# Cross attention and a mixture of experts on one core: score work of the second group moved into the first step, and operand forms changed

## The chip, the cores and the metric

The kernel runs on one core of one Trainium2 chip. The metric is the device time of one execution in microseconds (us), lower is better. The kernel before took 248.23 us (median of three runs, 245.85 to 248.69). Engines are named as in the profile: PE (TensorE), DVE (VectorE), ACT (ScalarE), POOL (GpSimd) and SP (SyncE, which here only issues DMAs).

## The reference, cut to what matters

```python
# x, ctx: (16, 128, 128) = batch, sequence, features
x = x + xattn(layernorm(x), ctx, ctx, Wq, bq, Wk, bk, Wv, bv, Wo, bo)
x = x + ffn(layernorm(x), Wr, Wg, Wu, Wd, Sg, Su, Sd)

def xattn(q, k, v, ...):                     # 16 heads of 8 features
    scores = einsum('bhid,bhjd->bhij', Q, K) / sqrt(8) + alibi_bias(128)
    return einsum('bhij,bhjd->bhid', softmax(scores), V) @ Wo.T + bo

def ffn(x, ...):                             # 16 experts of 64, top 2, and a shared one of 128
    probs = softmax(x @ Wr); top_p, top_i = top_k(probs, 2)
    routed = sum over e of (silu(x @ Wg[e]) * (x @ Wu[e])) @ Wd[e] * c[e]
    return routed + (silu(x @ Sg) * (x @ Su)) @ Sd
```

## The kernel before

The batch of 16 sequences is cut into eight groups of two (NG = 8, NB = 2 sequences b of 128 rows, T = 256). Each engine has its own program, written out by hand, and semaphores join them. Work is pipelined over groups: a step handles up to four of them at once, `step(f, a, p, q, abuf)`: the experts of group f, the attention of group a = f+1, the q/k/v products of p = f+2 and the first layer norm of q = f+3. The first step is `step(None, 0, 1, 2, 0)`, attention of group 0 with no expert work beside it; then `run_steps` issues `step(0, 1, 2, 3, 1)`, four steps in a hardware loop, two more, and a tail for group 7. Within a step the order on each engine is the order of the code. Nothing on an engine overtakes an instruction that waits.

Attention of a group and sequence b runs as: `scores(a, b, g)` on PE, four heads at a time (g = 0..3) into the two PSUM banks `ps_s`; `row_max` on DVE for each (L881), so that PE can't be more than two ahead; `max_high` (L887) and `max_low` (L891) split the 16 maxima into two float16 parts, `nsplit`; `shift_T` on PE transposes them, `shift_copy` on ACT copies them and `shift_rows` sends them by DMA as two extra rows of the stacked queries (`s_nm`); only then `scores_T` on PE forms the transposed and shifted scores, ACT takes exponentials (L668), `weigh_values` and `values_T` form the weighted values, `row_sums` and `normalise` divide, `attention_T` and `project_out` project, and `residual1` adds the residual (L914). Then `norm2_stats`, `norm2_mean` on DVE, the power -1/2 on POOL (L1179, L1183) and `norm2` on DVE (L933, `x2n`) give the input of the experts. Sequence 0's `norm2` is the step's last but three DVE call; sequence 1's comes at the start of the next step, and `expert_in_T` on PE waits for it.

The expert part: `up(f, c)` on PE for nine chunks c in high and low float32r parts of the weights (`wg_hi`, `wg_lo` and so on), tanh on ACT, `gate` and `hidden` on DVE, multiplication by the routing weights on POOL (`weigh_experts`, L1211: `hid` times `crep`, both in SBUF, 128x512), `down` on PE. `weigh_experts(f, 0)` stands on POOL between the two `inverse_deviation2` calls. The routing weights go to DRAM (`weights_out`, a DMA from ACT's queue, L676) and come back spread over the partitions (`spread_weights`, SP). The low parts of the weights are formed once, in the first step (`weights_low`, L1002 to L1004, DVE). `keep_clock` issues PE transposes whose results are unused.

Which operands lie where matters below: `x_all`, `x1_all`, `mv2`, `rstd2`, `nmax`, `nsplit`, `zero`, `hid`, `crep`, `xb` and the weights are in SBUF; what begins with `ps_` is in PSUM.

## Time and profile before

| | before |
|---|---|
| median of three runs | 248.23 us (245.85 to 248.69) |
| the profiled execution, own time | 247.91 us |
| its span | 246.1 us |
| PE busy / DVE / ACT / POOL | 222.8 / 181.0 / 111.2 / 65.9 us |
| granted PE clock, mean | 0.986 of full |

The span is what the trace covers; 1.8 us of the execution's time lie around it. Times in the rows count from the span's start. A row of the timeline gives start, duration, engine, line, operation, output and inputs, and in brackets how long the engine was idle before it and what ended the wait. The first step is about 16.6 to 37.9 us, the second 37.9 to 62.3, and each step after that takes 26.5 us or a little more.

### The profile page before, as it was taken

The page shows a single profiled execution, that of the slowest core. Times are in us where ns is not written, and L with a number is a line of the kernel's source. Part 1 is how long each engine was busy: PE and PEld are TensorE (multiplying, and loading weights), DVE is VectorE, ACT ScalarE, POOL GpSimd, SP SyncE. Part 2 cuts the span into 40 slices and gives each one's busy share as a digit, 9 for nine tenths or more (in the row PEclk, how much of TensorE's full clock was granted, in tenths as well). Part 3 has the DMA queues.
Part 4 walks back from the last instruction along what each step waited for, and adds up shares of the span by engine and source line. Part 5 has one row for each costly group of instructions (what it writes and reads, how often), then busy time and mean ns, then how long its engine had stood idle before and what let it go on. Part 6 is the DMA issues. An engine that isn't in the chain of part 4 may idle for free.

```text
span 246.1 us, 6073 instructions
## 1 busy us (share of the span) xinstructions
PE 222.8 (91%) x1979; PEld 180.0 (73%) x1979; DVE 181.0 (74%) x644; ACT 111.2 (45%) x260; POOL 65.9 (27%) x119
## 2 busy tenths in 40 slices
PE   2886978899899998999899989999999889989995
PEld 2773556668698777877787869877887669768985
DVE  4699348965997589847996589658983899356882
ACT  8574445365325632464336432563256323752320
POOL 3500014010741047013811074105700380017000
PEclk9998699999999999999999999999999999999999
DMA  5651792425024510624051602460164300260000
GB/s 153 187 99 62 151 289 79 112 45 160 1 72 75 147 52 23 122 79 119 0 127 23 186 0 76 68 175 17 32 113 106 93 0 4 51 149 0 3 21 21
DMA packets 13078, 20.23 MB, mean 82 GB/s; under 512 B 2800, under 2 KB 9440, under 8 KB 12544
## 3 DMA queue, kind: packets, MB, share of 16 engines
q1 hardware_dynamic: 11856, 18.52, 31.1%
q10 hardware_dynamic: 1200, 1.43, 2.0%
q8 instruction: 12, 0.20, 0.3%
q14 instruction: 10, 0.08, 0.1%
HBM read 16.03 MB, written 3.78 MB: 81 GB/s over the span
## 4 chain that ended last, share of the span: by engine, by line
PE 44%; issue 30%; POOL 11%; DVE 8%; DMA 4%; ACT 1%; POOLq 0%; DVEq 0%; SPq 0%; ACTq 0%
PE ps_m L504 8%; PE ps_up L478 7%; POOL hid L1211 6%; PE ps_pv L413 4%; DVE nmax L881 4%; PE ps_st L384 4%; PE ps_st L394 4%; PE ps_up L483 3%; PE ps_pv L420 2%; POOL rstd L1183 2%; DMA stacks_sb<-qk_dram 2%; PE ps_up L292 2%; PE ps_st L446 1%; DMA ident<-in_c_ident 1%; DVE tg L987 1%
## 5 line engine op out<-in xcount | busy, mean ns | idle before, releaser
L987 DVE SCALAR_TENSOR_TENSOR tg<-th,ps_up 128x256 f32<-128x256 f32 x72 | 29.8, 414 | 29.3 <-ACT th L713 29.3
L668 ACT ACTIVATE probs<-ps_st 128x512 f32<-128x512 f32 x64 | 38.1, 598 | 25.1 <-PE ps_st L394 20.3
L713 ACT ACTIVATE th<-ps_up 128x256 f32<-128x256 f32 x72 | 27.6, 384 | 42.1 <-PE ps_up L483 42.0
L504 PE MATMUL ps_m<-wd_sb,hid 128*128 128x128 f32 x288 | 44.1, 280 | 0.6 <-DVE x_all L914 0.6
L881 DVE TENSOR_REDUCE nmax<-ps_s 128x4 f32<-128x512 f32 x64 | 42.6, 680 | 0.5 <-issue 0.4
L504 PEld LDWEIGHTS ps_m<-wd_sb,hid 128*128 128x128 f32 x288 | 37.6, 191 | 1.4 <-DVE x_all L914 1.0
L1211 POOL TENSOR_TENSOR hid<-hid,crep 128x512 f32<-128x512 f32 x28 | 35.1, 1274 | 3.8 <-DVE x2n L933 3.8
L993 DVE TENSOR_TENSOR hid<-tg,ps_up 128x256 f32<-128x256 f32 x72 | 29.8, 413 | 1.0
L478 PE MATMUL ps_up<-x_hi,wg_hi 128*128 128x256 f32 x72 | 26.6, 369 | 2.6 <-DVE hid L993 2.5
L351 PE MATMUL ps_s<-stacks_sb 96*128 96x128 f16 x256 | 23.8, 220 | 3.0 <-DVE nmax L881 2.5
L1179 POOL TENSOR_TENSOR ve<-mv,eps_sb 128x1 f32<-128x1 f32 x16 | 3.1, 192 | 84.7 <-DVE mv L926 84.7
L394 PE MATMUL ps_st<-stacks_sb 98*128 98x128 f16 x256 | 25.6, 225 | 0.0
L394 PEld LDWEIGHTS ps_st<-stacks_sb 98*128 98x128 f16 x256 | 19.1, 100 | 7.2 <-issue 0.9
L351 PEld LDWEIGHTS ps_s<-stacks_sb 96*128 96x128 f16 x256 | 16.5, 97 | 9.3 <-DVE nmax L881 6.5
L1171 POOL TENSOR_TENSOR ve<-mv,eps_sb 128x2 f32<-128x2 f32 x8 | 1.6, 195 | 70.7 <-DVE mv L840 70.7
L483 PE MATMUL ps_up<-x_lo,wg_hi 128*128 128x256 f32 x72 | 20.1, 279 | 0.0
L478 PE MATMUL ps_up<-x_hi,wg_lo 128*128 128x256 f32 x72 | 20.1, 279 | 0.0
L478 PE MATMUL ps_up<-x_hi,wu_hi 128*128 128x256 f32 x72 | 20.1, 279 | 0.0
L478 PE MATMUL ps_up<-x_hi,wu_lo 128*128 128x256 f32 x72 | 20.1, 279 | 0.0
L483 PE MATMUL ps_up<-x_lo,wu_hi 128*128 128x256 f32 x72 | 20.0, 278 | 0.0
L413 PE MATMUL ps_pv<-probs,v_aug 128*32 128x384 f32 (+1 forms) x256 | 17.1, 385 | 0.5 <-ACT probs L668 0.5
L478 PEld LDWEIGHTS ps_up<-x_hi,wg_hi 128*128 128x128 f32 x72 | 13.6, 190 | 4.8 <-DVE hid L993 2.4
(133 smaller groups left out, 442.3 us busy)
## 6 DMA issues: line engine op xcount, KB each, us to landing
crep<-cw_dram SPq DMA_DIRECT2D x28, 256.0 KB, 4.4
stacks_sb<-qk_dram SPq DMA_DIRECT2D x32, 128.0 KB, 3.7
qk_dram<-qk_parts SPq DMA_DIRECT2D x16, 128.0 KB, 1.8
out_y<-x_all SPq DMA_DIRECT2D x8, 128.0 KB, 4.0
wg_sb<-in_wgT ACTq DMA_DIRECT2D x1, 576.0 KB, 3.4
wu_sb<-in_wuT ACTq DMA_DIRECT2D x1, 576.0 KB, 3.4
wd_sb<-in_wd SPq DMA_DIRECT2D x1, 576.0 KB, 3.9
x_all<-in_x SPq DMA_DIRECT2D x2, 256.0 KB, 4.2
```

The source lines that it names most:

```text
L351: last = mm(bank[:, o:o + P], qs[buf][0:ZROWS, h, b * P:(b + 1) * P], ks[buf][0:ZROWS, h, b * P:(b + 1) * P], start=(g > 0), stop=True, sk ...
L394: last = mm(bank[:, o:o + P], ks[buf][:, h, b * P:(b + 1) * P], qs[buf][:, h, b * P:(b + 1) * P], start=first, stop=True, skip_group_check ...
L413: last = mm(ps_pv[32 * c:32 * c + 32, r * 3 * P:(r * 3 + n) * P], v_aug[:, b, r, c, :], probs[:, b, h * P:(h + n) * P], start=True, stop=T ...
L478: mm(ps_up[c % 2][:, k, :], w[:, c, :], x2_hi[:], start=(k == 0 and n == 0), stop=False, skip_group_check=True)
L483: last = mm(ps_up[c % 2][:, k, :], hi[:, c, :], x2_lo[:], start=False, stop=True, skip_group_check=True)
L504: last = mm(ps_dn[:, b * P:(b + 1) * P], hid[:, buf, c, b * P:(b + 1) * P], wd_sb[:, c, :], start=(c == 0 and b == 0), stop=(c == SHARED), ...
L668: fn(probs[:, b, g * HG * P:(g + 1) * HG * P], ps_st[g % 2][:], ACT.Exp).then_inc(exp_sb, 1)
L713: fn(th[:, c % 2, :], ps_up[c % 2][:, 0, :], ACT.Tanh, scale=0.5).then_inc(tanh_sb, 1)
L881: v.tensor_reduce(nmax[:, b, HG * g:HG * g + HG], ps_s[g % 2][:].rearrange("p (h j) -> p h j", h=HG), AX_X, ALU.max, negate=True).then_inc ...
L987: v.scalar_tensor_tensor(out=tg[:, c % 2, :], in0=th[:, c % 2, :], scalar=1.0, in1=ps_up[c % 2][:, 0, :], op0=ALU.add, op1=ALU.mult).then_ ...
L993: v.tensor_tensor(hid[:, buf, c, :], tg[:, c % 2, :], ps_up[c % 2][:, 1, :], ALU.mult).then_inc(hid_sb, 1)
L1211: g.tensor_tensor(h2, h2, c2, ALU.mult).then_inc(hc_sb, 1)
```

## The change

1. The first step (`first`) now also issues the score products of group 1 for (b, g) = (0,0) to (1,1) and the row maxima for (0,0) to (1,0), and group 1's first transposed maxima. The second step (`second`) issues what is left of them, so that group 1's scores no longer stand in front of and between the expert products of group 0. The order of the rest in the two steps changes with it. Group 1's value product goes to another PSUM bank (`ps_v1`, in `ps_up[0]`). More `keep_clock` transposes stand in the first step (1, 2, 2, 2, 3, 3 and 8 where before there were 6).
2. `weights_low` moves from DVE to POOL.
3. Both norms (`norm1`, `norm2`) become `scalar_tensor_tensor` with the reciprocal deviation as a second tensor (broadcast from one column) in place of `tensor_scalar` with two per-partition scalars; `max_high` becomes a `tensor_tensor` addition of a broadcast zero in place of a casting copy.
4. The DMA of the routing weights to DRAM is issued by SP in `spread_weights`, not by ACT.

From the third step on the order on PE and DVE is the same as before; only the forms of 3 and the issuer of 4 differ.

```diff
@@ run_steps
-            step(0, 1, 2, 3, 1)
+            second(0, 1, 2, 3, 1)
@@ SP
             def spread_weights(f):
+                sp.wait_ge(cwT_sb, f + 1)
+                sp.dma_start(cw_dram[f], cwT[:]).then_inc(s_cwd, 16)
                 sp.wait_ge(s_cwd, 16 * f + 16)
@@ ACT
-            def weights_out(f):
-                act.wait_ge(cwT_sb, f + 1)
-                act.dma_start(cw_dram[f], cwT[:]).then_inc(s_cwd, 16)
@@ PE
+            def first():
...
+                shift_T(0, 0)
+                scores(0, 1, 1, 0)
+                keep_clock(3)
+                project_v(1)
+                scores(0, 1, 2, 0)
+                keep_clock(3)
+                scores(0, 1, 3, 0)
+                keep_clock(8)
+                scores_T(0, 0, 0, 0)
+                shift_T(0, 1)
...
+                weigh_values(0, 0)
+                scores(1, 0, 0, 1)
+                scores_T(0, 1, 2, 0)
+                values_T(0, 0)
+                scores(1, 0, 1, 1)
+                scores_T(0, 1, 3, 0)
+                scores(1, 0, 2, 1)
+                attention_T(0, 0, None)
+                weigh_values(0, 1)
+                project_out(0, 0)
+                scores(1, 0, 3, 1)
+                values_T(0, 1)
+                scores(1, 1, 0, 1)
+                attention_T(0, 1, None)
+                scores(1, 1, 1, 1)
+                project_x(2)
+                project_out(0, 1)
+                shift_T(1, 0)
+
+            def second(f, a, p, q, abuf):
+                project_q(p)
+                project_k(p)
+                scores(a, 1, 2, abuf)
+                expert_in_T(f)
+                scores(a, 1, 3, abuf)
+                up(f, 0)
+                router(f)
+                up(f, 1)
+                shift_T(a, 1)
+                up(f, 2)
+                scores_T(a, 0, 0, abuf, f=f)
+                up(f, 3)
+                scores_T(a, 0, 1, abuf, p=p)
+                second_half(f, a, p, q, abuf)
@@ DVE
-                    last = v.tensor_scalar(xn[:, b, :], x_all[:, p * NB + b, :], mv1[:, b, 0:1], rstd1[:, b:b + 1],
-                                           ALU.subtract, ALU.mult)
+                    last = v.scalar_tensor_tensor(out=xn[:, b, :], in0=x_all[:, p * NB + b, :], scalar=mv1[:, b, 0:1],
+                                                  in1=rstd1[:, b:b + 1].to_broadcast([P, P]), op0=ALU.subtract, op1=ALU.mult)
...
-                v.tensor_copy(nsplit[:, b, 0, :], nmax[:, b, :]).then_inc(nh_sb, 1)
+                v.tensor_tensor(nsplit[:, b, 0, :], nmax[:, b, :], zero[:].to_broadcast([P, H]), ALU.add).then_inc(nh_sb, 1)
...
-                v.tensor_scalar(x2n[:, b, :], x1_all[:, a * NB + b, :], mv2[:, b, 0:1], rstd2[:, b:b + 1],
-                                ALU.subtract, ALU.mult).then_inc(x2n_sb, 1)
+                v.scalar_tensor_tensor(out=x2n[:, b, :], in0=x1_all[:, a * NB + b, :], scalar=mv2[:, b, 0:1],
+                                       in1=rstd2[:, b:b + 1].to_broadcast([P, P]), op0=ALU.subtract,
+                                       op1=ALU.mult).then_inc(x2n_sb, 1)
@@ POOL, called in the first step between copy_ctx(1) and inverse_deviation1(2)
+            def weights_low():
+                pool.wait_ge(act_setup, 4)
+                g.tensor_tensor(wg_lo[:], wg_sb[:], wg_hi[:].bitcast(F32), ALU.subtract).then_inc(lo_sb, 1)
+                g.tensor_tensor(wr_lo[:], wr_sb[:], wr_hi[:].bitcast(F32), ALU.subtract).then_inc(lo_sb, 1)
+                pool.wait_ge(act_setup, 5)
+                g.tensor_tensor(wu_lo[:], wu_sb[:], wu_hi[:].bitcast(F32), ALU.subtract).then_inc(lo_sb, 1)
```

Two places of the order, as the programs have it (operation, output and inputs by name, elements of the output; a row may stand for several alike). DVE in the first step, from group 0's first row maxima to the first reciprocal of row sums, before:

```order
L881 TENSOR_REDUCE nmax<-ps_s 128x4 x4
L887 CAST nsplit<-nmax 128x16
L891 TENSOR_TENSOR nsplit<-nmax,nsplit 128x16
L862 SCALAR_TENSOR_TENSOR qk_parts<-ps_st,bqk_sb,qk_parts 128x256 x2
L1002 TENSOR_TENSOR wg_lo<-wg_sb,wg_hi 128x1152
L1003 TENSOR_TENSOR wu_lo<-wu_sb,wu_hi 128x1152
L1004 TENSOR_TENSOR wr_lo<-wr_sb,wr_hi 128x16
L896 RECIPROCAL rden<-ps_pv 128x16
```

(these begin with sequence 1's maxima), and after the change, from the end of sequence 0's maxima on:

```order
L966 TENSOR_TENSOR nsplit<-nmax,zero 128x16
L970 TENSOR_TENSOR nsplit<-nmax,nsplit 128x16
L941 SCALAR_TENSOR_TENSOR qk_parts<-ps_st,bqk_sb,qk_parts 128x256 x2
L960 TENSOR_REDUCE nmax<-ps_s 128x4 x4
L966 TENSOR_TENSOR nsplit<-nmax,zero 128x16
L970 TENSOR_TENSOR nsplit<-nmax,nsplit 128x16
L960 TENSOR_REDUCE nmax<-ps_s 128x4
L975 RECIPROCAL rden<-ps_pv 128x16
```

The low parts of group 1's keys and queries (`qk_parts`) moved ahead of sequence 1's four row maxima, the three weight subtractions left the engine, and a row maximum of group 1 stands ahead of the reciprocal. POOL in the first step, after the change:

```order
L1315 COPY ctx_g<-ctx_all 128x256
L1319 TENSOR_TENSOR wg_lo<-wg_sb,wg_hi 128x1152
L1320 TENSOR_TENSOR wr_lo<-wr_sb,wr_hi 128x16
L1322 TENSOR_TENSOR wu_lo<-wu_sb,wu_hi 128x1152
L1282 TENSOR_TENSOR ve<-mv,eps_sb 128x2
```

Before, the deviation of group 2 (`ve`) followed the copy directly.

## Rows read from the trace of the kernel before

**Rows 1.** The page's busy times: us, share of the span, instructions

```profile
PE 222.8 (91%) x1979; PEld 180.0 (73%) x1979; DVE 181.0 (74%) x644; ACT 111.2 (45%) x260; POOL 65.9 (27%) x119
```

**Rows 2.** Busy time by stretch: PE, PEld, DVE, ACT, POOL; then clock, DMA share, GB/s

```profile
16.60:23.60 7.00, 4.58 (x41) 2.93 (x41) 6.75 (x15) 4.18 (x5) 0.00 (x0) 0.90 0.27 88
23.60:37.90 14.30, 12.61 (x103) 8.30 (x103) 6.58 (x28) 6.53 (x13) 1.70 (x4) 0.81 0.81 215
37.90:62.30 24.40, 22.16 (x203) 16.68 (x202) 18.69 (x77) 13.01 (x31) 4.09 (x11) 1.00 0.36 85
88.80:115.30 26.50, 25.50 (x237) 20.90 (x237) 20.95 (x79) 11.85 (x30) 8.62 (x15) 1.00 0.34 80
```

**Rows 3.** Timeline, all engines, the seam between two steps of the loop

```profile
88.55 1.26 POOL L1211 TENSOR_TENSOR hid<-hid,crep 128x512 f32<-128x512 f32 x1
88.62 1.27 DVE L933 TENSOR_SCALAR x2n<-x_all,mv,rstd 128x128 f32 x1 [0.20 <-POOL rstd L1183]
88.65 0.49 PE L433 MATMUL ps_m<-wT,attnT 128*128 128x128 f32 x2
...
89.82 0.28 DVE L914 TENSOR_TENSOR x_all<-ps_m,xb 128x128 f32 x1
...
91.32 0.40 PE L351 MATMUL ps_s<-stacks_sb 96*128 96x128 f16 x4 [0.15 <-DVE nmax L881]
...
93.36 0.39 PE L478 MATMUL ps_up<-x_hi,wg_hi 128*128 128x256 f32 x1 [0.38 <-DVE hid L993]
```

**Rows 4.** Timeline, POOL and DVE, a few us later in the same step

```profile
92.08 3.75 POOL L1211 TENSOR_TENSOR hid<-hid,crep 128x512 f32<-128x512 f32 x3 [0.54 <-DVE x2n L933]
94.86 0.99 DVE L887 CAST nsplit<-nmax 128x16 f16<-128x16 f32 x1
95.79 0.46 POOL L1193 TENSOR_TENSOR xb<-x_all,bo_rep 128x128 f32<-128x128 f32 x1
96.11 0.17 DVE L891 TENSOR_TENSOR nsplit<-nmax,nsplit 128x16 f16<-128x16 f32 x1
```

**Rows 5.** One line's instructions: shortest, median, longest in ns, first and last start

```profile
L933 DVE TENSOR_SCALAR x2n<-x_all,mv,rstd x16: 335/406/1287, 37.9 to 224.0; 128x128 f32<-128x128 f32 x8, 128x128 f32 x8
L887 DVE CAST nsplit<-nmax x16: 174/174/1002, 20.0 to 206.9; 128x16 f16<-128x16 f32 x16
L891 DVE TENSOR_TENSOR nsplit<-nmax,nsplit x16: 167/174/175, 20.2 to 207.1; 128x16 f16<-128x16 f32 x16
```

**Rows 6.** Timeline of the first step and the start of the second

```profile
22.29 1.16 ACT L717 ACTIVATE wu_hi<-wu_sb 128x1152 fp32r<-128x1152 f32 x1 [1.35 <-issue]
22.93 0.17 DVE L887 CAST nsplit<-nmax 128x16 f16<-128x16 f32 x1
23.23 0.87 DVE L862 SCALAR_TENSOR_TENSOR qk_parts<-ps_st,bqk_sb,qk_parts 128x256 f16<-128x256 f32 x2
...
24.02 1.35 DVE L1002 TENSOR_TENSOR wg_lo<-wg_sb,wg_hi 128x1152 fp32r<-128x1152 f32 x1
...
29.02 0.39 PE L384 MATMUL ps_st<-slope_hi,dist 128*128 128x512 f16 x1
...
32.26 0.26 DVE L896 RECIPROCAL rden<-ps_pv 128x16 f32<-128x16 f32 x1 [5.55 <-PE ps_pv L420]
...
39.98 0.47 DVE L933 TENSOR_SCALAR x2n<-x_all,mv,rstd 128x128 f32<-128x128 f32 x1 [0.37 <-POOL rstd L1183]
40.37 0.68 DVE L881 TENSOR_REDUCE nmax<-ps_s 128x4 f32<-128x512 f32 x1
```

**Rows 7.** Timeline of the second step: a shift DMA and the routing DMA

```profile
49.85 0.62 ACTq L672 DMA_DIRECT2D stacks_sb<-nmT  x1
...
50.04 0.36 PE L478 MATMUL ps_up<-x_hi,wg_hi 128*128 128x256 f32 x1
...
52.31 0.36 ACTq L676 DMA_DIRECT2D cw_dram<-cwT  x1
...
52.85 0.38 PE L384 MATMUL ps_st<-slope_hi,dist 128*128 128x512 f16 x1 [0.23 <-DMA stacks_sb<-nmT]
```

More of the change, by code:

```diff
@@ L588, in _ @@
             keep_clock(36)
-            step(None, 0, 1, 2, 0)
-            run_steps(pe, step)
+            first()
+            run_steps(pe, step, second)
             f, last = NG - 1, (NG - 1) % 2
@@ new lines, in first @@
+            def first():
+                qk_high(1)
+                shift_copy(0, 0)
+                shift_rows(0, 0, 0)
+                up_weights_high()
+                shift_copy(0, 1)
+                shift_rows(0, 1, 0)
+                for b in range(NB):
+                    for g in range(NHG):
+                        exponential(0, b, g)
+                        if (b, g) == (1, 1): values_copy(0, 0)
+                attention_copy(0, 0)
+                values_copy(0, 1)
+                attention_copy(0, 1)
+                x_T(2)
+                shift_copy(1, 0)
+                shift_rows(1, 0, 1)
@@ new lines, in second @@
+            def second(f, a, p, q, abuf):
+                qk_high(p)
+                x2_high(f)
+                tanh(f, 0)
+                act.wait_ge(s_wd, 16)
+                fn(wd_sb[:], wd_sb[:], ACT.Copy, scale=0.5).then_inc(wd_half, 1)
+                tanh(f, 1)
+                shift_copy(a, 1)
+                shift_rows(a, 1, abuf)
+                router_exp(f)
+                tanh(f, 2)
+                exponential(a, 0, 0)
+                tanh(f, 3)
+                second_half(f, a, q)
@@ L795, in _ @@
             fill(ks[1][ZROWS:AROWS], ones16)
-            step(None, 0, 1, 2, 0)
-            run_steps(act, step)
+            first()
+            run_steps(act, step, second)
             f = NG - 1
@@ new lines, in first @@
+            def first():
+                for g in range(NHG):
+                    row_max(0, 0, g)
+                max_high(0, 0)
+                max_low(0, 0)
+                qk_low(1, 1)
+                qk_low(1, 0)
+                for g in range(NHG):
+                    row_max(0, 1, g)
+                max_high(0, 1)
+                max_low(0, 1)
+                row_max(1, 0, 0)
+                row_sums(0, 0)
+                normalise(0, 0)
+                row_max(1, 0, 1)
+                norm1_stats(2)
+                norm1_mean(2)
+                row_max(1, 0, 2)
+                residual1(0, 0)
+                row_max(1, 0, 3)
+                norm2_stats(0, 0)
+                max_high(1, 0)
+                norm2_mean(0, 0)
+                max_low(1, 0)
+                row_sums(0, 1)
+                normalise(0, 1)
+                row_max(1, 1, 0)
+                norm1(2)
+                norm2(0, 0)
+                residual1(0, 1)
+                norm2_stats(0, 1)
+                norm2_mean(0, 1)
+                values(1)
@@ new lines, in second @@
+            def second(f, a, p, q, abuf):
+                row_max(a, 1, 1)
+                norm2(f, 1)
+                row_max(a, 1, 2)
+                x2_low(f)
+                row_max(a, 1, 3)
+                max_high(a, 1)
+                max_low(a, 1)
+                router_max(f)
+                gate(f, 0)
+                router_shift(f)
+                hidden(f, 0, 1 - abuf)
+                qk_low(p, 1)
+                qk_low(p, 0)
+                gate(f, 1)
+                hidden(f, 1, 1 - abuf)
+                route(f, 0)
+                route(f, 1)
+                gate(f, 2)
+                route(f, 2)
+                hidden(f, 2, 1 - abuf)
+                second_half(f, a, p, q, abuf)
@@ new lines, in step @@
+            def step(f, a, p, q, abuf):
+                row_max(a, 0, 0)
+                norm2(f, 1)
+                row_max(a, 0, 1)
+                gate(f - 1, 8)
+                hidden(f - 1, 8, abuf)
+                x2_low(f)
+                row_max(a, 0, 2)
+                row_max(a, 0, 3)
+                max_high(a, 0)
+                gate(f, 0)
+                max_low(a, 0)
+                hidden(f, 0, 1 - abuf)
+                if p is not None: qk_low(p, 1)
+                row_max(a, 1, 0)
+                if p is not None: qk_low(p, 0)
+                gate(f, 1)
+                row_max(a, 1, 1)
+                hidden(f, 1, 1 - abuf)
+                router_max(f)
+                row_max(a, 1, 2)
+                router_shift(f)
+                gate(f, 2)
+                hidden(f, 2, 1 - abuf)
+                row_max(a, 1, 3)
+                route(f, 0)
+                max_high(a, 1)
+                route(f, 1)
+                max_low(a, 1)
+                route(f, 2)
+                second_half(f, a, p, q, abuf)
@@ L1107, in _ @@
             v.memset(cwT_r[:].bitcast(F32), 0.0).then_inc(dve_pads, 1)
-            step(None, 0, 1, 2, 0)
-            run_steps(dve, step)
+            first()
+            run_steps(dve, step, second)
             f, last = NG - 1, (NG - 1) % 2
```

352 lines of the change are left out of this document (150 added, 202 removed).

## The prediction

> **What bounds the kernel now.** I read the page first: PE is busy 91% of the span, DVE 74%, POOL 27%, with the clock at full from 38 us on [rows 1, 2]. Then the busy time by stretch [rows 2]: a step of the loop is 26.5 us with 25.5 us of PE, so there PE sets the pace and can only gain its own waits, about 1 us a step. The first step is different: PE is busy 4.6 of 7.0 and 12.6 of 14.3 us, at a clock of 0.90 and 0.81, DVE only 6.6 of 14.3 us in its later part; this is a chain of latencies. The second step (24.4 us) has 22.2 us of PE. Last I read the timeline where PE waits. At the seam of two steps [rows 3] DVE's `norm2` for sequence 0 starts 0.07 us after POOL's product of `hid` and `crep` and takes 1.27 us, where its shortest takes 0.335 [rows 5]. Everything DVE does next is late: the residual at 89.82, the row maxima, the second norm. PE's waits at 91.32 and 93.36 are on that chain. A little later the 16-column cast of `max_high` takes 0.99 us and ends at 95.85, when POOL's three products end (95.83) [rows 4]; its usual length is 0.174 [rows 5]. In the whole trace `norm2` is caught like this seven times (once a seam) and the cast six times.
>
> **The change, part by part.** My sum starts from the profiled execution's own 247.9 us; the median is 0.3 us above it.
>
> *Routing DMA on SP.* ACT loses an issue of 0.36 us in seven steps [rows 7]. Its next instruction is an exponential, and PE at 52.85 was waiting for the shift DMA, not for it; in the loop no PE wait on an exponential is listed at that place. SP stands idle after its stack loads, so the transfer starts when it did. The routing weights are wanted by POOL only at the step's end, some us after they land. 0 us; at most 0.1 either way per step if the issue were seen, so 0 to -0.7 in all.
>
> *Low weight parts on POOL.* DVE gives up 2.9 us (two of 1.35 us and a short one) in a gap: it then idles 5.55 us until 32.26 [rows 6]. Gain from that alone 0. On POOL the price comes from its two rows: 1.26 us for 512 columns [rows 3] and 0.46 for 128 [rows 4], 2.1 ns a column, so 1152 columns cost 1.26 + 640 x 0.0021 = 2.6 us each. `wg_lo` follows ACT's high parts, about 15.6 to 18.3, with nothing on DVE that reads two SBUF tensors. `wu_lo` can start when ACT's `wu_hi` ends, 22.29 + 1.16 = 23.45 [rows 6], and ends at about 26.1. PE wants it after 40 us: hidden. POOL's next work comes after 33 us: nobody queues behind. What may not be hidden is DVE's `max_high` at that moment, priced below.
>
> *Scores of group 1 in the first step.* PE's part is six score products of 0.25 to 0.45 us, in waits it has anyway. The weight is on DVE: a row maximum costs 0.68 us [rows 6], five move into the first step. The 5.55 us gap takes only one, because PE reaches group 1's scores behind `weigh_values` (about 31 us); another 1.7 us gap takes two. The rest delays the chain of group 0's second sequence: `normalise` by 0.8 us, and `project_out(0, 1)` now stands on PE behind `project_x(2)`, which waits for `norm1(2)`, queued behind five row maxima. Following DVE's queue instruction by instruction I get the second `norm2` at 41.6 in place of 39.98 [rows 6], 1.6 us late. After it two row maxima are left where there were seven, 5 x 0.68 = 3.4 us less. That is 1.8 us for DVE; from PE's next four `up` products on, tanh and the routing chain come last, which keep part of it. I take **-1.0 us**. Bounds: 0 (the delay eats it) and -2.5 (nothing is kept back; also -0.2 to -0.4 for the shift DMA's wait at 52.85 [rows 7], which goes since that DMA is issued earlier).
>
> *Other operand forms.* This decides. The new forms read two tensors from SBUF. Alone they cost about the same as before: 0.335 for `norm2`, 0.17 for 16 columns [rows 5]. What they cost beside a POOL instruction that reads SBUF has no clean row. Lower bound: `max_low` has two SBUF tensors and took 0.17 us at 96.11 while `xb` was running [rows 4], no longer than elsewhere [rows 5]; if that is the answer, nothing blocks. Upper bound: the cast and the old norm, which wait for POOL's instruction to end. But look at the ends: the blocked cast ends 0.02 us after POOL's product (95.85 against 95.83), and `max_low` ends 0.03 us after the first `xb` (96.28 against 96.25) [rows 4]. The row that seems free ends just where a blocked one would. The six like it have the same spacing, so it excludes nothing. I take the upper bound, as the nearest in size and place: same tile, same POOL product, still both ends in SBUF, and one that must bring two tensors in at once.
>
> The Trainium skill, SBUF — State Buffer, "Who interferes with whom", says that a DVE instruction with two SBUF inputs contends with a GpSimd instruction that reads SBUF, since its second input comes through the shared read interface. It speaks against this part of the change; by it the sum would be the one of the blocked case below, without it the free case.
>
> Blocked: `norm2` ends some 0.07 us later than now at each of seven seams, since its 128 columns come at one a cycle (1152 in 1.35 us [rows 6]), not at two: **+0.5 us**. And a new collision in the first step. `qk_low`, 0.87 us [rows 6], now stands ahead of sequence 1's row maxima, so `max_high(0, 1)` is due at 22.93 + 0.87 = 23.8, inside `wu_lo` on POOL (23.5 to 26.1). It would end at 26.2. Behind it: `max_low`, `shift_T(0, 1)` on PE (with `scores_T(0, 0, 1)` queued behind), ACT's copy (with the exponentials behind), then the DMA, 3.0 us from issue to use (49.85 to 52.85) [rows 7]. So `scores_T(0, 1, 0)` starts at about 30.1 in place of 28.7, against 29.02 now [rows 6]: 1.4 us lost, of which I take **+1.2** (0 if POOL starts after DVE, 1.5 at most).
>
> Sum, blocked: 247.9 - 1.0 + 0.5 + 1.2 = **248.6 us**, own range 246.5 to 250.5.
>
> **The rivals.**
>
> *Free case.* DVE's norm isn't held. It ends at 88.95; the residual then starts when `project_out` ends (88.65 + 0.49, so 89.2) in place of 89.82: 0.64 us [rows 3]. PE's waits at 91.32, before 92.58 and at 93.36 (0.3 to 0.5 us each) can take that up. The cast is 0.8 us shorter, which removes PE's 0.25 us wait for `nsplit`. Together 0.9 us, close to all of PE's 1 us of idle time a step [rows 2]; PE's products follow without a gap from there. Seven seams, the last a little less: -6.0. With -1.0 for the order: 247.9 - 7.0 = 240.9 us. For it: `max_low` never longer than 175 ns [rows 5]. Against it: the spacing of the ends.
>
> *Half case.* The two engines take turns on what they share, so that norm and cast last some 0.6 us: half of 6.0 us, and no long stop in the first step: about 244.
>
> *Slower.* In the blocked case PE stands from about 25 to 26.4 us in the first step, and the clock falls to its lower level (1.2 of 2.4 GHz) for the rest of it. Already now it is at 0.81 on average in 23.6 to 37.9 [rows 2], where PE had been busy only 4.6 of the 7 us before. If the low level lasted from 24 to 39 us, some 10 us of work at full clock would need up to 20, against the 12.6 us busy now; 5 us of it on the chain: 253.6. [...] The eight more `keep_clock` products speak against it.
>
> *The order does nothing.* DVE's load in the two steps is the same but for the gaps; if all three gaps are lost the time is 1 us above each case. This changes no sign, it is in the ranges.
>
> **How the numbers follow.** Blocked 0.52, free 0.34, half 0.10, slower 0.04. The likeliest gives 248.6 us, with its own range 246.5 to 250.5. A measurement tells about 2% here, that is below 243.3 or above 253.2. Faster: the free case and a third or so of the half case, 0.38. Slower: 0.04, and blocked with everything against it, 0.01. Same: 0.57. The range must hold the free case too: 240.0 to 250.5, which leaves out the lower third of the free case and the slow one.
>
> **What would show it.** Norm2 at the seams: 1.3 us again (blocked) or about 0.3 (free). `max_high` beside the three products: 0.9 or 0.17. In the first step: `max_high(0, 1)` starting at about 23.8 and lasting 2.3 us, or 0.17. The first `up` product of chunk 4 at about 48.7 us instead of 50.04 [rows 7] if the order works as worked out and nothing blocks. A loop step of 26.5 us (blocked) or 25.6 (free). I am wrong if a norm that isn't blocked leaves the step at 26.5 us, or if the first two steps end over 2.5 us earlier.

## The result and the profile after

The changed kernel takes 250.56 us (median of four executions, 250.48 to 250.71), the kernel before on the same chip 248.16. The ratio is 1.0107, with a 95% interval of 1.0075 to 1.0139: 2.4 us slower by the medians, 2.7 by the ratio, and clearly not zero. Forecast were 248.6 us and a range up to 250.5, so the time lies 0.06 us outside it. Medians below count every execution; the ratios leave out those that took over 1.5% longer than the fastest of the same kernel.

The page of the profile after, its first lines: span, then busy us, share and instructions of each engine.

```profile
span 248.9 us, 6097 instructions
PE 224.1 (90%) x1994; PEld 181.8 (73%) x1994; DVE 181.9 (73%) x641; ACT 110.8 (45%) x260; POOL 71.3 (29%) x122
```

POOL has the 5.4 us of the low parts more than in [rows 1]; the others are as they were. Busy time by stretch, with the same columns as [rows 2], and four shorter stretches behind it:

```profile
16.60:23.60 7.00, 6.09 (x60) 4.83 (x61) 6.32 (x14) 3.72 (x5) 1.75 (x2) 1.00 0.37 126
23.60:37.90 14.30, 10.85 (x107) 6.76 (x106) 6.43 (x14) 6.49 (x13) 3.10 (x3) 0.88 0.70 195
37.90:62.30 24.40, 21.27 (x183) 16.34 (x181) 17.45 (x75) 13.09 (x30) 4.17 (x11) 0.93 0.37 85
88.80:115.30 26.50, 25.43 (x238) 20.83 (x237) 21.09 (x78) 11.71 (x30) 8.64 (x14) 1.00 0.42 101
43.00:45.00 2.00, 1.03 (x11) 0.67 (x9) 1.72 (x5) 1.19 (x3) 1.91 (x5) 1.00 0.03 8
...
47.00:49.00 2.00, 2.00 (x10) 1.66 (x10) 1.96 (x7) 1.06 (x3) 0.00 (x0) 0.50 0.00 0
...
30.00:33.00 3.00, 2.82 (x17) 1.69 (x21) 0.00 (x0) 1.36 (x4) 0.00 (x0) 0.50 0.59 159
```

A step of the loop is what it was. The first two steps are not: PE is at its lower level (1.2 of 2.4 GHz) from 30 to 33 us and again from 47 to 50, where before it was at full from 30 us on. The kernel before has a low stretch of its own, but an earlier one, as the same columns of its trace show:

```profile
24.00:28.00 4.00, 4.00 (x23) 2.88 (x22) 2.72 (x4) 0.98 (x2) 0.00 (x0) 0.50 0.57 150
```

POOL's first pair of `hid` products in each step marks the seams, the places where one step ends and the next begins. They lay at 61.88, 88.55 ... 221.00 us before, and lie at 64.12, 90.92 ... 223.74 now: 2.24 us are lost ahead of the first seam, and 0.5 us over the six steps behind it. So the question is the first two steps.

The forecast rows came out nearly to the digit. One line's instructions (shortest, median, longest in ns), the norm and the high part of the row maxima, as in [rows 5]:

```profile
L1012 DVE SCALAR_TENSOR_TENSOR x2n<-x_all,mv,rstd x16: 347/400/1352, 41.0 to 226.8; 128x128 f32<-128x128 f32 x16
L966 DVE TENSOR_TENSOR nsplit<-nmax,zero x16: 156/176/2599, 20.6 to 209.7; 128x16 f16<-128x16 f32 x16
```

Timeline of the collision in the first step, and of a seam (compare [rows 3, 4]):

```profile
24.13 2.61 POOL L1322 TENSOR_TENSOR wu_lo<-wu_sb,wu_hi 128x1152 fp32r<-128x1152 f32 x1 [5.78 <-ACT wu_hi L774]
24.18 2.60 DVE L966 TENSOR_TENSOR nsplit<-nmax,zero 128x16 f16<-128x16 f32 x1
26.81 0.17 DVE L970 TENSOR_TENSOR nsplit<-nmax,nsplit 128x16 f16<-128x16 f32 x1
...
27.04 0.23 PE L371 MATMUL ps_pv<-ident,nsplit 128*32 128x128 f16 x1 [2.10 <-DVE nsplit L970]
...
90.92 1.27 POOL L1329 TENSOR_TENSOR hid<-hid,crep 128x512 f32<-128x512 f32 x1
90.99 1.34 DVE L1012 SCALAR_TENSOR_TENSOR x2n<-x_all,mv,rstd 128x128 f32<-128x128 f32 x1 [0.19 <-POOL rstd L1294]
```

An addition of 16 columns takes 2.60 us because POOL's 1152 columns take 2.61, and PE waits 2.10 us for it. Its clock doesn't fall right behind that wait: it is at full until 29.5 us and at 0.50 from 30, behind two shorter waits for ACT's exponentials (0.95 us before 28.93 and 0.26 before 30.18). The fall comes without the collision too (experiments 2 and 3). At the seam the norm is held as before, 0.07 us longer.

### The profile page after: what moved, and what is told of

The parts are those of the page before. It is cut to its first block, busy times and chain, and to the rows that moved or that the text cites. A ratio compares the mean times of both kernels' runs of the same rounds, so it can differ in the third digit from the quotient of the medians.

```text
span 248.9 us, 6097 instructions
## 1 busy us (share of the span) xinstructions
PE 224.1 (90%) x1994; PEld 181.8 (73%) x1994; DVE 181.9 (73%) x641; ACT 110.8 (45%) x260; POOL 71.3 (29%) x122
## 4 chain that ended last, share of the span: by engine, by line
PE 42%; issue 29%; POOL 11%; DVE 11%; DMA 4%; ACT 1%; DVEq 0%; POOLq 0%; SPq 0%; ACTq 0%
PE ps_m L516 8%; PE ps_up L490 7%; POOL hid L1329 6%; DVE nmax L960 5%; PE ps_pv L424 4%; PE ps_st L405 4%; PE ps_st L395 3%; PE ps_up L495 3%; POOL rstd L1294 2%; PE ps_pv L431 2%; DMA stacks_sb<-qk_dram 2%; PE ps_st L457 1%; DMA ident<-in_c_ident 1%; DVE nsplit L966 1%; DVE tg L1067 1%
## 5 line engine op out<-in xcount | busy, mean ns | idle before, releaser
L362 PEld LDWEIGHTS ps_s<-stacks_sb 96*128 96x128 f16 x256 | 17.1, 98 | 8.1 <-DVE nmax L960 5.1
```

The costliest lines, as they stand in the source:

```text
L362: last = mm(bank[:, o:o + P], qs[buf][0:ZROWS, h, b * P:(b + 1) * P], ks[buf][0:ZROWS, h, b * P:(b + 1) * P], start=(g > 0), stop=True, sk ...
```

## The experiments

Times are medians; the ratio is to the kernel before on the same chip in the same call. What each edit leaves out of the computation: nothing, all fifteen compute the whole. Experiments 1, 2, 3 and 11 take the change apart, the others test what it did to the waits and the clock. "Full clock" means a mean granted clock of 0.998 or more over an execution.

### 1. The operand forms alone

```diff
-                v.tensor_scalar(x2n[:, b, :], x1_all[:, a * NB + b, :], mv2[:, b, 0:1], rstd2[:, b:b + 1],
+                v.scalar_tensor_tensor(out=x2n[:, b, :], in0=x1_all[:, a * NB + b, :], scalar=mv2[:, b, 0:1],
+                                       in1=rstd2[:, b:b + 1].to_broadcast([P, P]), op0=ALU.subtract,
...
-                v.tensor_copy(nsplit[:, b, 0, :], nmax[:, b, :]).then_inc(nh_sb, 1)
+                v.tensor_tensor(nsplit[:, b, 0, :], nmax[:, b, :], zero[:].to_broadcast([P, H]), ALU.add).then_inc(nh_sb, 1)
```

> The kernel before with only the new operand forms of the norms and of max_high. Theory A (a DVE instruction with two SBUF tensors waits for a POOL instruction that reads SBUF, as the old forms did): norm2 at the seams 1.34 us, max_high beside the three products 0.9 to 1.0, time of before plus 7 x 0.07 = 248.7 us. Theory B (only the old forms wait): norm2 0.35, max_high 0.18, 242 to 243 us.

Measured: 248.42 us, ratio 1.0018 [0.9986, 1.0049]. The norm's longest is 1.355 us, `max_high` beside the three products 1.0 us. The seams go from 61.82 to 221.49, 159.67 us for six steps against 159.12 before: +0.55. The free case is out, and the +0.5 us of the sum stands. That size comes from the seams; the ratio's interval alone would also hold 0.

### 2. The collision taken away

```diff
                 pool.wait_ge(act_setup, 5)
+                pool.wait_ge(ns_sb, 2)
                 g.tensor_tensor(wu_lo[:], wu_sb[:], wu_hi[:].bitcast(F32), ALU.subtract).then_inc(lo_sb, 1)
```

> The changed kernel with POOL's wu_lo started only after max_low(0, 1), so that nothing of POOL runs beside max_high(0, 1). If that collision is the main cost of the change: max_high(0, 1) 0.17 us, first step 1.2 to 2.3 us shorter, time 248.3 to 249.4 us. If the clock or the order is: under 0.5 us back, 250.1 us or more.

Measured: 249.64 us, ratio 1.0071 [1.0040, 1.0102]: 0.9 us less than the full change. The pair of rows now reads, in the timeline of this kernel:

```profile
23.57 0.17 DVE L966 TENSOR_TENSOR nsplit<-nmax,zero 128x16 f16<-128x16 f32 x1
23.77 0.17 DVE L970 TENSOR_TENSOR nsplit<-nmax,nsplit 128x16 f16<-128x16 f32 x1
24.09 2.62 POOL L1323 TENSOR_TENSOR wu_lo<-wu_sb,wu_hi 128x1152 fp32r<-128x1152 f32 x1 [6.16 <-DVE nsplit L970]
```

So the collision costs about 0.9 us, of 1.2 taken, and 1.5 us remain with it gone. The size is a rough one: the two ratios' intervals overlap, and at a mean clock of 0.985 or 0.986 alone the difference is 0.4 us (250.2 in four executions here, 250.56 in the four of the full change). The trace agrees with less than 1.2: from the start of `max_high(0, 1)` to that of `scores_T(0, 1, 0)` it is 6.00 us with the collision and 5.35 (23.57 to 28.92) without, since the wait for the shift's DMA was behind it anyway.

### 3. The order alone

The changed kernel with the old forms, the low parts back on VectorE and the routing DMA back on ScalarE; what is left is the order of the first two steps.

> Only the order of the first two steps changed; operand forms, the weights' low parts on DVE and the routing DMA on ACT as before. If the order is worth what I forecast: 1 us under before, 247.2 us. If the gap of PE ahead of the first expert products lets the clock fall there (the changed kernel ran 47 to 49 us at half clock), the order costs: 0.5 to 1 us over before, 249 us.

Measured: 248.80 us, ratio 1.0050 [1.0017, 1.0083]. The order, forecast to give 1.0 us, costs 1.2. The timeline of PE shows where it stands still, and for how long its clock is low afterwards:

```profile
29.69 0.38 PE L393 MATMUL ps_st<-slope_hi,dist 128*128 128x512 f16 x1 [1.92 <-issue]
...
30.66 0.53 PE L393 MATMUL ps_st<-slope_hi,dist 128*128 128x384 f16 x1
```

and the busy time by stretch (columns as in [rows 2]):

```profile
28.00:30.00 2.00, 0.31 (x2) 0.22 (x3) 0.00 (x0) 0.57 (x2) 0.00 (x0) 1.00 0.04 3
30.00:32.00 2.00, 2.00 (x17) 1.24 (x16) 0.00 (x0) 0.60 (x1) 0.00 (x0) 0.50 0.46 147
32.00:34.00 2.00, 2.00 (x20) 0.80 (x20) 0.00 (x0) 0.79 (x2) 0.00 (x0) 0.65 0.76 181
```

The second shift's DMA is issued at 25.57 and first used at 29.69, 4.1 us later, where I had taken 3.0. The profile names no releaser for PE's wait there ("issue"); that it is the shift's DMA is borne out by experiment 5, where the shift goes out earlier and the wait is gone. PE does 0.31 us of work in 28 to 30 us, and then works at half clock. From 34 us on this trace is at full clock, and so is that of experiment 2: the second fall, at 47 to 50 us, stands in the trace of the full change alone.

### 4. The norm set free by a wait

In the kernel before, POOL's first pair of products waits for the norm that it used to hold.

```diff
                     if f is not None:
+                        pool.wait_ge(x2n_sb, 2 * a + 1)
                         weigh_experts(f, 0, 1 - abuf)
```

> The kernel before, where POOL's product for chunks 0 and 1 waits for norm2 of sequence 0, so that the norm goes first at each of the seven seams and POOL's product starts 0.4 us later. If the wait for POOL is worth what I put in the free case for the norm (0.65 us a seam): 243.5 to 244.5 us. If PE's waits at the seam have another cause: 247.5 us or more. The casts stay caught, so their 0.25 us a step stays.

Measured: 245.99 us, ratio 0.9919 [0.9889, 0.9949]. No norm lasts longer than 0.47 us. The seam interval shrinks by 0.25 to 0.45 us, so what this edit gives is some 0.3 us a seam, where the free case had 0.65. It isn't quite the free case: POOL's product now comes later and is itself in the way of the second deviation. The timeline of POOL and DVE at one seam:

```profile
89.59 1.27 POOL L1211 TENSOR_TENSOR hid<-hid,crep 128x512 f32<-128x512 f32 x1 [0.64 <-DVE x2n L933]
90.33 0.18 DVE L926 BATCH_NORM_AGGREGATE mv<-stats 128x2 f32<-128x6 f32 x1
90.82 0.19 POOL L1179 TENSOR_TENSOR ve<-mv,eps_sb 128x1 f32<-128x1 f32 x1
```

`ve` starts 0.31 us after its input is there, 0.07 in the kernel before. What a norm that isn't held is worth while POOL doesn't wait for it, no run shows.

### 5. and 6. The wait for the shift: moved, and filled

Both start from the order alone. The first brings the second shift forward:

```diff
-                keep_clock(8)
+                shift_T(0, 1)
+                keep_clock(6)
                 scores_T(0, 0, 0, 0)
-                shift_T(0, 1)
...
-                qk_low(1, 1)
-                qk_low(1, 0)
                 for g in range(NHG):
                     row_max(0, 1, g)
                 max_high(0, 1)
                 max_low(0, 1)
+                qk_low(1, 1)
+                qk_low(1, 0)
```

> The kernel with the new order alone (e3_order, +1.2 us over before), with two moves in its first step: TensorE issues shift_T(0,1) before scores_T(0,0,0) instead of behind it, and VectorE works off row_max(0,1,*) and max_high/max_low(0,1) before the low parts of group 1's queries and keys. So the second shift goes out to its DMA as early as in the kernel before. Theory L (the order loses its time in the wait for the second shift: issued at 25.57, used at 29.69, with TensorE idle for 1.9 us and its granted clock at 0.50 to 0.65 from 30 to 34): the shift's DMA is issued at 23.5 to 24.3, scores_T(0,1,0) starts at 27.5 to 28.5, and the seams (POOL's first hid pair of each step) lie 1.0 to 2.0 us earlier than 62.68, 89.36, 115.91; ratio to before 0.997 to 1.001. Rival Q (the time goes later, between 38 and 54 us, where the second norm of group 0 is queued behind the waits of project_x(2), and the first up product follows it): the row maxima come earlier, but the seams stay within 0.4 us of 62.68 and 89.36; ratio 1.004 to 1.006.

Measured: 249.51 us, ratio 1.0069 [1.0042, 1.0097]: no gain over the order alone, and its seams lie 0.7 us later (63.39 against 62.68). `scores_T(0, 1, 0)` does start at 27.92, as hoped. But the next group's stacks start later, and PE stands there instead:

```profile
29.29 1.07 PE L422 MATMUL ps_pv<-probs,v_aug 128*32 128x384 f32 x16
33.14 0.39 PE L357 MATMUL ps_s<-slope_hi,dist 128*128 128x512 f16 x1 [2.78 <-DMA stacks_sb<-qk_dram]
```

Both transfers come out of the same few microseconds of VectorE. Whichever goes second is late. The new order needs both early; the old one needed only the shift.

The second leaves the wait and fills it:

```diff
                 scores_T(0, 0, 3, 0)
+                keep_clock(14)
                 scores_T(0, 1, 0, 0)
```

> The kernel with the new order alone (e3_order), with 14 idle transposes (keep_clock, 14 x 0.13 = 1.8 us at the full clock) on TensorE between scores_T(0,0,3) and scores_T(0,1,0), in the wait for the second shift's DMA. The wait stays, only TensorE doesn't idle in it. If the fall of the clock is what the wait costs (from 30 to 34 us TensorE was busy all the time at 0.50 and 0.65 of full speed, so it did in 4.0 us the work of 2.3): granted clock 1.00 from 30 to 34 us, row_max(1,0,0) at 33.0 to 33.6 instead of 34.31, seams 0.7 to 1.5 us earlier than 62.68 and 89.36, ratio 0.999 to 1.002. If the wait itself is what counts (1.9 us of a chain that ends at the row maxima): clock full but seams within 0.4 us, ratio 1.004 to 1.006.

Measured: 247.20 us, ratio 1.0004 [0.9960, 1.0048]: 1.6 us less than the order alone by the medians, 1.1 us by the ratios. In its profile the clock is at full throughout and `row_max(1, 0, 0)` starts at 32.24 instead of 34.31. By its size the fall of the clock looks like all that the order cost. It isn't: the kernel before has a fall as well, and filling its waits gives as much (experiment 15); at full clock in both, the new order is still behind (experiment 11).

### 7. and 8. A form that isn't held, and both remedies

```diff
-                v.tensor_copy(nsplit[:, b, 0, :], nmax[:, b, :]).then_inc(nh_sb, 1)
+                v.tensor_reduce(nsplit[:, b, 0, :], nmax[:, b, :].unsqueeze(2), AX_X, ALU.max).then_inc(nh_sb, 1)
```

> The kernel before, with only the copy nmax -> nsplit high written as a reduction over an axis of length one (same values), in place of a copy from SBUF to SBUF. Theory P (VectorE is held by GpSimd only in forms with two SBUF tensors and in the fast mode that a plain SBUF copy uses): the reduction is not held, x16 at about 170/180/250 ns instead of 174/176/1002 for the copies, the seven that lay beside the hid triple (94.86 0.99) fall to about 0.2; ratio 0.997 to 1.000, since the chain of a seam ran over hid pair and norm and not over this copy. Rival (any VectorE instruction that writes or reads SBUF while GpSimd works is held): unchanged 1.0 us, ratio 0.999 to 1.002. If the copy did lie on the chain: up to 7 x 0.8 = 5.6 us less, ratio 0.977.

Measured: 246.64 us, ratio 0.9952 [0.9926, 0.9978]. The timeline beside the three products, and the groups of both lines over the whole trace:

```profile
91.38 3.76 POOL L1211 TENSOR_TENSOR hid<-hid,crep 128x512 f32<-128x512 f32 x3 [0.54 <-DVE x2n L933]
...
94.17 0.17 DVE L887 TENSOR_REDUCE nsplit<-nmax 128x16 f16<-128x16 f32 x1
94.61 0.57 DVE L891 TENSOR_TENSOR nsplit<-nmax,nsplit 128x16 f16<-128x16 f32 x1
```

```profile
L887 DVE TENSOR_REDUCE nsplit<-nmax x16: 169/170/171, 19.8 to 205.1; 128x16 f16<-128x16 f32 x16
L891 DVE TENSOR_TENSOR nsplit<-nmax,nsplit x16: 166/176/572, 20.0 to 205.3; 128x16 f16<-128x16 f32 x16
```

A reduction of one tensor is never held (at most 171 ns). The subtraction behind it, two tensors from SBUF, now comes while POOL is still at work and is held: it ends at 95.18, POOL's products at 95.14. In [rows 4] it came when POOL's three products had ended and only `xb` was at work, which ended 0.03 us before it, so its 0.17 us could not tell. That decides what the prediction had argued from the spacing of the ends.

> The kernel before, with the reduction of e7_max_high and the wait of e4_hid_after (GpSimd's first hid pair of a step waits for the first norm of that step, ratio 0.992 alone). With the hid pair later, the hid triple behind it also moves later by about 1 us and meets the high part of the row maxima. If the held copy costs something in this order: ratio 0.985 to 0.990, seams at intervals of 26.2 us instead of 26.4. If not: 0.990 to 0.994, the same as e4_hid_after.

Measured, with this edit and that of experiment 4: 244.31 us, ratio 0.9863 [0.9804, 0.9923].

### 9. The changed kernel mended, and 12. with all remedies

The changed kernel with the edits of experiments 2 and 6:

> The changed kernel with two mendings, each tried before by itself: 14 idle transposes (keep_clock) in the wait for the second shift's DMA (e6_filled: 1.6 us less than e3_order by the medians), and wu_lo on GpSimd only behind max_low(0,1) (e2_wu_late: 0.9 us less than the changed kernel). Theory S (the +2.4 us are the sum order +1.2, collision +0.9, held norms +0.5, and the order's part is mostly the clock that falls in that wait): 250.56 - 0.9 - 1.6 = 248.1, range 247.3 to 249.0, ratio 0.997 to 1.004, granted clock 1.00 from 28 to 34 us. Rival (the low parts on GpSimd, the routing DMA on SyncE's queue or another part costs something of its own that only shows in the full change): 249.5 or more, ratio over 1.005.

Measured: ratio 1.0005 [0.9984, 1.0026], that is 247.7 us against 247.62, from seven of eleven executions; the median of all eleven is 248.30. By the seven the sum of the parts holds. The executions fall apart by mean clock: 247.4 us in five at 1.00, 248.5 in two at 0.993, and 250.9 to 251.3 in four at 0.979. In these four the mended kernel takes as long as the full change did. One of these four was profiled; its clock is low from 40 to 50 us, behind the stretch where PE waits for norms:

```profile
36.00:40.00 4.00, 2.69 (x25) 1.90 (x22) 3.35 (x16) 0.86 (x3) 1.26 (x3) 1.00 0.56 182
40.00:50.00 10.00, 9.82 (x42) 7.95 (x42) 7.24 (x26) 4.10 (x11) 2.12 (x6) 0.53 0.08 24
```

The wait doesn't decide it alone: the profiled execution of experiment 6 has the same one (PE 2.68 of 4.00 us busy from 36 to 40) and stays at full clock. Why the clock falls there in some executions stays open. Experiments 6, 13 and 14, with the same order, have a few such executions too (2 of 10, 2 of 10, 1 of 4).

> The changed kernel with the two mendings of e9_after_mended, and with what made before faster in e8_both: the high part of the row maxima as a reduction of one tensor, and GpSimd's first hid pair waiting for the first norm. If the full change with its faults taken away is worth more than the kernel before with the same two edits (the order then wins its forecast 1.0 us): 243.3 or less. If the order is worth nothing (e6_filled at full clock 246.7 against 245.7 for before at full clock): 244.3 to 245.5, ratio 0.984 to 0.990; and then e10_fills should be faster than this by 1 to 2 us.

Measured, with the edits of experiments 4 and 7 as well: 243.43 us, ratio 0.9833 [0.9804, 0.9862], between the two cases expected. Its executions at full clock take 243.3 us; the old order with the same two edits took 242.3 in the one execution at full clock (experiment 8), and 242.8 with fills (experiment 10). So with its faults taken away the full change is still 0.5 us or more behind, of which the moved parts may be 0.3 (experiment 11).

### 10. and 15. The clock of the kernel before

Idle transposes in the first step of the old order, in the waits for the row maxima (two behind each of five score products, eight ahead of `shift_T(0, 1)`), on top of experiment 8 and alone:

```diff
                 if as_: scores(a, 0, 2, abuf)
+                if not fs: keep_clock(2)
...
                     if not fs:
+                        keep_clock(8)
                         shift_T(a, 1)
```

> e8_both (the kernel before with the single-input reduction and the wait of GpSimd for the first norm, 244.31 us) with idle transposes between the scores of the first step (five times 2) and 8 ahead of shift_T(0,1), where TensorE waited 1.22 us for VectorE. In the profile of before the clock stood at 0.54 from 22 to 24 us and 0.50 from 24 to 28; the one execution of before with a mean clock of 1.0 took 245.71 us against 248.15 for those at 0.986, that of e8_both at 0.999 took 242.32 against 244.34. Theory C (those idle gaps at 20 to 23.4 us make the clock fall, and a run in which it doesn't fall is 2 us shorter): mean clock 0.993 to 1.000 in nearly every execution, median 242.0 to 243.3, ratio 0.975 to 0.982. Rival (the time lost at half clock is hidden by DMAs and VectorE, the fast runs were fast for another reason, for instance quicker loads): clock at 1.0 but median 243.8 to 244.8, ratio 0.984 to 0.988. Third: the transposes themselves delay the scores: slower than 244.8.

> The kernel before with the idle transposes of e10_fills alone. Theory C (before loses 2 us in most executions to the clock that falls at 22 to 28 us): mean clock 0.993 to 1.000 in nearly all, median 245.5 to 246.5, ratio 0.990 to 0.995. Then the three edits in e10_fills are -2.0 (GpSimd waits for the norm), -1.4 (the reduction) and -1.9 (the clock), whose sum is -5.3 against -4.9 measured. Rival (clock only helps where the held norms are gone): 247.5 or more.

Measured: 242.77 us on top of experiment 8, ratio 0.9796 [0.9773, 0.9818], the fastest kernel here. Alone 246.20 us, ratio 0.9934 [0.9916, 0.9953]. The mean clock was 0.998 or more in all fourteen executions. Before, in the same stretch as below, PE had 4.00 us of busy time at a clock of 0.50. In the kernel with the fills alone:

```profile
24.00:28.00 4.00, 3.62 (x38) 2.13 (x40) 2.52 (x3) 2.61 (x5) 0.00 (x0) 1.00 0.56 150
```

The kernel before, 94 executions over the four calls of the experiments, sorted by its mean clock, says the same:

| mean granted clock | executions | median us |
|---|---|---|
| 0.986 | 53 | 248.1 |
| 0.992 or 0.993 | 38 | 247.6 |
| 0.999 or 1.000 | 3 | 245.7 |

### 11. The two moved parts alone

Low parts on GpSimd and routing DMA by SyncE, all else as before.

> The kernel before with only the two moved parts of the change: the low parts of the gate, up and router weights on GpSimd (wg_lo and wr_lo as soon as the high part of the gate weights is there, wu_lo behind wu_hi) and the DMA of the routing weights issued by SyncE. The order of the first steps and the forms of the norms and row maxima stay as before. Forecast for both together: 0, ratio 0.997 to 1.003, seams within 0.3 us of 61.88 and 88.55 at equal clock. Rival (SyncE's queue comes later to the routing DMA than ScalarE's, so that crep is late for the hid triple of each step): crep lands later and the interval of the seams grows by 0.1 us or more, ratio over 1.003. Other rival (copying wg_lo on GpSimd holds VectorE's memset or casts between 14 and 22 us, and the first step is later by up to 1 us): seam intervals the same and all seams later by one amount.

Measured: 248.25 us, ratio 1.0018 [1.0005, 1.0031]; at the clock of 0.986, 248.4 against 248.1. Some 0.3 us at equal clock, 0.45 by the ratio, which I can't place: the seam intervals are the same and the crep loads take 4.4 us in both. `max_high(0, 1)` (22.99) is through before `wu_lo` starts (23.59), as the old order has it.

This kernel's profile caught an execution at full clock, so it can be laid beside that of experiment 6, also at full clock: the old order against the new, without the clock. Timeline of the old order (experiment 11), then of the new (experiment 6):

```profile
27.06 0.39 PE L387 MATMUL ps_st<-slope_hi,dist 128*128 128x512 f16 x1 [0.25 <-ACT probs L671]
...
38.07 0.47 DVE L931 TENSOR_SCALAR x2n<-x_all,mv,rstd 128x128 f32<-128x128 f32 x1 [0.37 <-POOL rstd L1174]
...
45.60 0.39 PE L387 MATMUL ps_st<-slope_hi,dist 128*128 128x512 f16 x1
```

```profile
29.23 0.38 PE L393 MATMUL ps_st<-slope_hi,dist 128*128 128x512 f16 x1 [0.48 <-issue]
...
41.41 0.38 DVE L1016 TENSOR_SCALAR x2n<-x_all,mv,rstd 128x128 f32<-128x128 f32 x1
...
46.18 0.39 PE L393 MATMUL ps_st<-slope_hi,dist 128*128 128x512 f16 x1
```

`scores_T(0, 1, 0)` is 2.2 us later, the second norm of group 0 3.3 us later, and `scores_T(1, 0, 0)`, behind the moved work, only 0.6 us later. The first seam keeps that (60.59 against 59.94). So the moved work gives back 2.7 us, as worked out, but it had been paid for with 3.3. What is left is 0.65 us; the medians of experiments 6 and 15, both with fills, are 1.0 us apart (247.20 and 246.20, on two chips).

### 13. and 14. The shift ahead of the stack loads

On experiment 6 (with 9 transposes for 14), SyncE issues the second pair of group 1's stack loads behind ScalarE's copy of the second shift:

```diff
+                elif isinstance(p, int) and p == 1:
+                    sp.wait_ge(nm_sb, 2)
                 sp.wait_ge(s_qd, 16 * p + 16)
```

> e6_filled (the new order alone, with idle transposes in the wait), but SyncE issues the second pair of group 1's stack loads (2 x 128 KB, issued at 24.0 and 24.4 there) only behind the copy of the second shift on ScalarE, and 9 idle transposes instead of 14. At full clock in both, e6_filled started scores_T(0,1,0) at 29.23, e11_moved (order of before) at 27.06; the shift's DMA was issued at 25.01 and took 4.2 us. Theory Q (those 4.2 us are the two stack loads that stand ahead of an 8 KB transfer in the 16 DMA engines; the order loses 2.2 us there): scores_T(0,1,0) at 27.9 to 28.4, the second norm of group 0 at 40.2 to 40.8 instead of 41.41, seam 0 at 59.4 to 60.0 instead of 60.59, median 1.0 us below e6_filled's best group (246.7) at full clock, so 245.4 to 246.2. Rival (the shift's DMA takes about 4 us wherever it stands): scores_T(0,1,0) still at 29.0 or later, no gain. Third: the held stack loads come too late for scores(1,0,0) at 31.6 and give the gain back.

Measured: 247.16 us, ratio 0.9974 [0.9943, 1.0005]; at full clock 246.2 against 246.8. The shift's DMA is issued at 25.51 and used at 29.18:

```profile
29.18 0.38 PE L395 MATMUL ps_st<-slope_hi,dist 128*128 128x512 f16 x1 [0.47 <-issue]
```

3.7 us instead of 4.2, and `scores_T(0, 1, 0)` starts hardly earlier than in experiment 6, where 27.9 to 28.4 were expected. But the edit did not take the second pair of loads out of the way, it put them beside the shift. SyncE issues them in the same moment as ScalarE issues the shift, and the DMA engines are at work until 28.0 us (columns as in [rows 2]):

```profile
25.50 0.77 SPq L236 DMA_DIRECT2D stacks_sb<-qk_dram  x2
25.51 0.63 ACTq L734 DMA_DIRECT2D stacks_sb<-nmT  x1
```

```profile
26.40:28.00 1.60, 1.17 (x14) 1.01 (x15) 0.86 (x2) 1.44 (x4) 0.00 (x0) 1.00 0.77 169
28.00:29.10 1.10, 0.71 (x7) 0.47 (x5) 0.00 (x0) 0.52 (x2) 0.00 (x0) 1.00 0.02 0
```

So what the loads cost the shift in all is not settled by this. The seam of this profile tells nothing, its clock fell at 40 us. Of the 2.2 us, 1.0 is that the shift is issued later (25.01 in experiment 6, 24.00 in experiment 11), the rest that it takes longer than the 3.1 us or less of the old order. What the last 0.6 us are, behind the first pair of loads and beside the second, stays open.

> e12_after_all (243.43 us) with the same two edits as e13_shift_ahead. Theory Q: 242.0 to 242.7, seam 0 at 60.1 to 60.7 instead of 61.23, level with e10_fills (242.77) or 0.5 us below it. Rival: 243.3 or more.

Measured: 244.12 us, ratio 0.9844 [0.9796, 0.9891], not better than experiment 12 by the medians (at full clock 243.3 in both), and 1.3 us above experiment 10.

## Why the prediction was wrong, and where it was right

*The mechanism that was to decide was right.* Blocked, not free: norms of 1.35 us (+0.5 us over the seams, forecast +0.5), `max_high(0, 1)` at 24.18 for 2.60 us (forecast 23.8, 2.3), `scores_T(0, 1, 0)` at 30.18 (forecast 30.1). The half case is out as well: each of the seven norms at the seams takes 1.34 or 1.35 us, none some 0.6. The collision was sized at 1.2 us and is worth about 0.9, 0.4 at equal clock (experiment 2). Part of its wait would have been there anyway, for the shift's DMA. The Trainium skill, SBUF — State Buffer, "Who interferes with whom", names the contention of a VectorE instruction with two SBUF inputs; every run here agrees with it (1.34 us, 2.60 us, 0.57 us where 0.34 and 0.17 are usual).

*The moved parts.* Both were forecast at 0 and came out at 0.3 to 0.45 us together (experiment 11).

*The failed step is "I take -1.0 us" for the order of the first two steps.* It cost 1.2 us (experiment 3), outside the bounds of 0 and -2.5 that I gave it. The first of these points is what made the term wrong; the other two are errors beside it:

1. I worked out the second norm at 41.6 and set it against 39.98, "1.6 us late". At full clock it comes at 41.41, nearly as worked out. But 39.98 is a time in which the kernel before had already lost its clock [rows 2, 0.81 on average]; at full clock it has that norm at 38.07. One side of the difference was made with the clock's fall in it and the other without. The lateness at equal clock is 3.3 us; between the traces of experiment 3 and the kernel before, both with a fall of the clock, it is 3.5 (43.48 against 39.98). The gain behind it (2.6 worked out, 2.7 measured) can't cover that: 0.65 us are lost even at full clock. With 38.07 in place of 39.98, the same working would have given about +0.9 us (3.5 late, less 2.6) in place of -1.0.
2. For the shift's DMA I took 3.0 us, from the second step [rows 7]. It stands behind four stack loads of 128 KB each there as well, but it is issued 2.2 us after the last two. In the order alone it is issued 1.0 us after them, and takes 4.1 us. The rows, first of the kernel before (the shift there at 49.85), then of experiment 3:

```profile
47.62 0.88 SPq L228 DMA_DIRECT2D stacks_sb<-qk_dram  x2
...
24.55 0.87 SPq L234 DMA_DIRECT2D stacks_sb<-qk_dram  x2
25.57 0.63 ACTq L731 DMA_DIRECT2D stacks_sb<-nmT  x1
```

This weighed little in the sum: without the collision I had `scores_T(0, 1, 0)` at 28.7, and experiment 2 has it at 28.92.
3. The clock fell in the wait that this makes. I had that mechanism only as the "slower" rival, at 253.6 us with a chance of 0.04, tied to the collision and to a low level lasting until 39 us. It fell for about 3 us, with the collision and without, and once more at 47 to 50 us in the full change. The first fall is a cost of the wait, but not of the new order against the old one: the kernel before is at 0.50 from 24 to 28 us, and fills give 1.7 us there (experiment 15), about what they give here (1.1 to 1.6, experiment 6).

As for the rivals' prices: the norm let go first gave 0.3 us a seam, where 0.65 was taken (experiment 4, in which POOL waits instead), and the free copy 1.2 us in all (experiment 7). Experiment 8 has both and takes 244.3 us; the free case was put at 240.9.

The parts add up: order +1.2, forms +0.45, collision +0.9, moved parts +0.3 to +0.45, together 2.85 to 3.0 us against 2.4 to 2.65 measured. The intervals of the first three ratios are 0.8 us wide to each side, so the sum agrees with the whole, but no single part is known better than that.

## What to carry to other kernels

When you replay a chain of waits by hand, replay the old order too, by the same rules: subtract two worked-out times or two measured ones, never one from the other, above all where the clock was low in one of them. Compare two orders at the same mean clock: here the old one lost as much by its fall (1.7 us) as the new one by its own. A filler in a wait that can't be avoided was worth more here (1.7 us) than the whole reordering. Where a small copy is held beside a GpSimd product, look for a form that isn't (here the reduction), and where a norm is held, let GpSimd wait for it: the two together gave 1.4%.

## What the runs showed of the hardware that I had not expected

- The same kernel takes 245.7, 247.6 or 248.1 us, and the groups go with its mean clock. A scatter of 1% that looked like noise hangs on one stretch of waiting of about 1 us (22.2 to 23.4 us): with it filled, all ten executions stayed at full clock (experiment 15). With the same wait unfilled the clock fell in most executions but not in all (the profiled ones of experiments 8 and 11 kept it).
- A reduction over an axis of length one copies 16 columns in 0.17 us and was not held by GpSimd in any of 16 instances, where a plain copy is held up to 1.0 us.
- A transfer of 8 KB took at most 2.6 us from issue to use when it was issued 3.2 us after the last stack loads (changed kernel, 27.60 to 30.18), at most 3.1 with none ahead (experiment 11), 3.0 when issued 2.2 us after them, 3.7 behind one pair and beside the other, and 4.1 to 4.2 when issued 1.0 us after the last of two pairs.
